# Loading the second and third group's queries and keys when the attention begins instead of within the projections

## The reference

```python
# layer 0: 16 heads of 16 numbers, causal
q, k, v = (proj(Wq), proj(Wk), proj(Wv))
q = q * cos + _rotate_half(q) * sin
k = k * cos + _rotate_half(k) * sin
scores = jnp.where(causal, min, einsum('bhqd,bhkd->bhqk', q, k) * scale)
out = einsum('bhqk,bhkd->bhqd', softmax(scores), v)
x = _layernorm(x + out @ Wo.T)
...
# layer 1: 16 pairs of heads of 8 numbers, not causal, rotary positions as well
attn1, attn2 = attend(q1, k1), attend(q2, k2)
a = attn1 - lam * attn2          # then an rms norm per head, and Wo
```

## Time and profile before

| | us |
|---|---|
| median of 3 runs | 3674.9 |
| lowest, highest | 3674.15, 3680.14 |
| the profiled execution, its own time | 3676.61 |
| its span, first to last instruction | 3674.9 |

### The profile page before, as it was taken

How to read it: one execution, slowest core, us unless ns; L and a number is a source line. 1 busy time by engine, 2 the same in 40 slices (tenths; PEclk the granted TensorE clock), 3 DMA queues, 4 the chain that set the end, 5 groups by cost and what they waited for, 6 DMA issues and landing times. The chain is left out here.

```text
span 3674.9 us, 63919 instructions
## 1 busy us (share of the span) xinstructions
PE 3200.6 (87%) x23832; PEld 1634.2 (44%) x23832; DVE 2804.8 (76%) x4740; ACT 2064.6 (56%) x4079; POOL 911.8 (25%) x1343
## 2 busy tenths in 40 slices
PE   7499999688598979999999999998567699998749
PEld 4244444444486523333333333333434354554626
DVE  7688884557577999999999999993654577775475
ACT  3078887155232339999999999998122133333110
POOL 4234344134333500000000000001144344444000
PEclk9689999788699969999999999999778799999679
DMA  5412220000000601010100101000012311100202
GB/s 179 124 40 69 54 55 22 23 1 1 24 1 21 187 25 28 20 28 20 28 20 20 27 20 28 20 20 4 9 57 91 119 29 45 48 2 4 98 20 81
DMA packets 77548, 157.14 MB, mean 43 GB/s; under 512 B 21336, under 2 KB 38752, under 8 KB 77120
## 3 DMA queue, kind: packets, MB, share of 16 engines
q1 hardware_dynamic: 73024, 148.97, 13.6%
q10 hardware_dynamic: 4224, 4.19, 0.3%
HBM read 87.76 MB, written 54.72 MB: 39 GB/s over the span
## 5 line engine op out<-in xcount | busy, mean ns | idle before, releaser
L600 ACT ACTIVATE L_parts<-L_attn_psS 128x512 f32<-128x512 f32 (+3 forms) x2816 | 1408.2, 574 | 138.1 <-PE L_attn_psS L727 100.7
L683 DVE TENSOR_REDUCE L_attn_tops<-L_attn_psM 128x2 f32<-128x1024 f32 x1152 | 1324.4, 1214 | 51.9 <-PE L_attn_psM L777 47.9
L777 PE MATMUL L_attn_psM<-L_K,L_Q 30*128 30x512 f32 (+4 forms) x2816 | 863.9, 488 | 62.5 <-DVE L_attn_tops L683 35.3
L727 PE MATMUL L_attn_psS<-L_Q,L_K 32*128 32x512 f32 (+4 forms) x2816 | 875.3, 472 | 2.0 <-ACT L_parts L600 0.7
L748 PE MATMUL L_attn_psS<-L_parts,L_attn_V 128*32 128x256 f32 (+1 forms) x10752 | 847.8, 387 | 5.8 <-ACT L_parts L600 0.6
L727 PEld LDWEIGHTS L_attn_psS<-L_Q,L_K 32*128 32x128 f32 (+1 forms) x2816 | 409.6, 184 | 548.3 <-ACT L_parts L600 258.3
L777 PEld LDWEIGHTS L_attn_psM<-L_K,L_Q 30*128 30x128 f32 (+1 forms) x2816 | 391.3, 189 | 109.5 <-DVE L_attn_tops L683 67.1
L748 PEld LDWEIGHTS L_attn_psS<-L_parts,L_attn_V 128*32 128x32 f32 x10752 | 214.4, 108 | 351.4 <-issue 182.1
L677 DVE CUSTOM_DVE_ANT_0 L_attn_psM<-L_attn_psM,L_attn_wide 128x384 f32<-128x384 f32 (+3 forms) x512 | 236.3, 521 | 18.8 <-PE L_attn_psM L777 18.2
L2312 ACT ACTIVATE x_E<-x_psS 128x512 f32<-128x512 f32 x256 | 138.9, 595 | 183.1 <-PE x_psS L2435 173.1
L2358 DVE TENSOR_REDUCE x_tops<-x_psM 128x2 f32<-128x1024 f32 x128 | 153.2, 1206 | 91.4 <-PE x_psM L2464 91.3
(11 more groups left out here) (343 smaller groups left out, 4093.4 us busy)
## 6 DMA issues: line engine op xcount, KB each, us to landing
parts_q<-L_parts SPq DMA_DIRECT2D x64, 256.0 KB
parts_k<-L_parts SPq DMA_DIRECT2D x64, 256.0 KB
L_Q<-parts_q SPq DMA_DIRECT2D x192, 64.0 KB
L_K<-parts_k SPq DMA_DIRECT2D x192, 64.0 KB
L_Q<-parts_q SPq DMA_DIRECT2D x64, 128.0 KB
L_K<-parts_k SPq DMA_DIRECT2D x64, 128.0 KB
queries<-x1p_qo SPq DMA_DIRECT2D x16, 512.0 KB
keys<-x1p_ko SPq DMA_DIRECT2D x16, 512.0 KB
```

Of the source, the lines that this page charges most:

```text
L600: act.activation(E[(4 * n + s) % (4 * RING)][:, c0:], psS[bank][:, c0:], ACT.Exp, scale=scale).then_inc(e_done, 1)
L683: dve.tensor_reduce(dst, src, AX, ALU.max).then_inc(m_read, 1)
L727: pe.matmul(psS[bank][:, c0:], K[g.slot][r:r + RH, c, kt * P:(kt + 1) * P], Q[g.slot][r:r + RH, c, q * HALF + c0:(q + 1) * HALF], start=Tr ...
L777: last = pe.matmul(psM[bank][:, j * HALF:j * HALF + n], Q[t.slot][r:r + TOP, c, qt * P:(qt + 1) * P], K[t.slot][r:r + TOP, c, h * HALF:h * ...
```

## The change

Between the halves of `project`, only group 0 is loaded, 16 DMAs instead of 48. In `attend`, SP's turns 1 and 2 also call `load_group`, without the two waits that the later groups have (the wait for `parts_out` stays at group 3, that for `s_done` at group 3 and later). So group 1 is loaded right after the mask (and in layer 1 the lambdas) are issued, since SP has nothing else in turn 0, and group 2 after the eight small DMAs of group 0's maxima. This holds for both layers.

```diff
--- before.py
+++ after.py
@@ -217,8 +217,7 @@
                         sp.wait_ge(blank, 6)
                         for k in range(4):
                             sp.wait_ge(out[k], OUT)
-                        for g in range(3):
-                            load_group(sp, keep, 2 * ne, g)
+                        load_group(sp, keep, 2 * ne, 0)
 
             @block.gpsimd
             def _(pool):
@@ -492,11 +491,12 @@
                     sp.dma_start(lam4[:], a[f"{tag}_lambda"].rearrange("(o k) d -> o k d", o=1).broadcast_to([P, 4, dh])).then_inc(lamin, 16)
 
                 def turn(t, new, last, old):
-                    if new and t.base >= 3:
+                    if new and t.base >= 1:
                         if t.base == 3:
                             for k in range(4):
                                 sp.wait_ge(parts_out[k], 256)
-                        sp.wait_ge(s_done, s_at[t.base - 3, NS - 1, 3] + 1)
+                        if t.base >= 3:
+                            sp.wait_ge(s_done, s_at[t.base - 3, NS - 1, 3] + 1)
                         load_group(sp, keep, dh, t.base)
                     if last:
```

## The result

| | before | after |
|---|---|---|
| median, us | 3680.64 (19 runs) | 3670.04 (19 runs) |
| lowest to highest | 3673.09 to 3693.76 | 3645.66 to 3687.77 |
| ratio, 95% interval | | 0.9965, 0.9952 to 0.9978 |
| the profiled execution's span | 3674.9 | 3669.7 |

By the ratio the change makes the kernel faster by 0.35%, 0.22 to 0.48%: about 12.9 us, between 8 and 18; the medians are 10.6 us apart. Forecast were 17.6 us and a time of 3657.3, in a range of 3652 to 3663; the measured 3670.04 lies outside. The miss of 12.7 us has two parts: the kernel before is at 3680.64 over 19 runs and not at the 3674.9 of the first three (5.7 us), and the difference of the medians is 10.6 us and not 17.6 (7.0 us).

The account below looks back on a forecast made before the run. The prediction took layer 0's second-half store drain, lengthened by loads ahead of it, as the bound. Layer 0's 16.4 us plus layer 1's 1.2 made 17.6, off the 3674.9 median: 3657.3 us, range 3652 to 3663.

Parts of the forecast that it names:

- The stores' drain gates the attention of layer 0: Layer 0: the first maxima start only once eight buffers of stores are drained; the change gains 16.4 us there.
- production has room to spare: Layer 0, second half: production and store issue allow the attention near 122, nearly 10 us before the drain at 131.6.
- ACT's stall is a symptom: Layer 0, unit 24: ACT's 18.98 us wait comes from the same queue, does not set the start, and shrinks to 0.4.
- the moved loads are covered: Attention: group 1 has 21 us of cover and group 2 has 19, so moving their loads costs nothing.
- layer 1 is worth about 1 us: Layer 1's projections: DVE's loss of 1.2 us is gained, with ends of nothing and 3.7 us.
- absorbed: Rival: the mask is late for its own reason or loads slow stores far more; gain under 7.3 us, 3668 to 3675; 4%.
- late loads: Rival: PE stands at turn 1 because group 1 has not landed, costing its lateness; landing at 186 gives 3682; 2%.
- the mask falls behind: Rival, layer 0: group 1's loads served beside the mask; total gain 9.4 us, 3665.5; sign: mask landing near 141; 6%.
- the stores are drained only at 91.6 + 40.0 = 131.6: Layer 0: store engines finish group 0's loads at 91.6, then need 40.0 us for 8.39 MB at 211 GB/s.
- The bound taken for slower stores: Layer 0, attention's begin: beside group 1's loads the stores fall to 157 GB/s for 8.2 us and lose 2.1 us.
- stores below 200 GB/s after 122: Layer 0, changed profile: named as a sign that the forecast is wrong, by contention.
- The attention begins near 122: Layer 0: production ends at 118.9, the last four stores' issue at 121.3, and the engines need 0.7 us to meet.

Follow-up runs that it names:

- half_stores: Changed kernel with half of layer 0's second-half stores left out (4.2 MB instead of 8.4), its last eight groups' loads reading the first eight's rows; 0.9923 of the kernel before.
- two_groups: Changed kernel with groups 0 and 1 loaded between the halves and group 2 in the attention, in both layers; ratio 0.9981 to the kernel before.
- load_after_four: Changed kernel with group 0's load moved behind the fourth buffer of the second half; ratio 0.9968 to the kernel before.
- spare_loads: Changed kernel with groups 1 and 2 also loaded between the halves, on their own semaphore, and again in the attention; ratio 1.0010 to the kernel before.
- after_again: The changed kernel measured and profiled again without an edit; ratio 0.9953 to the kernel before.

## Why the prediction was wrong in size

**What held.** The stores' drain gates the attention of layer 0 (half_stores), the loads between the halves stand ahead of it in the queue at about 8 us for a group (two_groups, 7.6 us), production has room to spare, ACT's stall is a symptom (load_after_four), the moved loads are covered (spare_loads, and no wait of PE), and layer 1 is worth about 1 us. The rivals "absorbed" and "late loads" did not happen. Nor did "the mask falls behind", although the mask, used at 143.48, came near the 141 that was its sign: in the four profiles with the change in layer 0 the mask is used 5.1 to 5.8 us after its issue, and in the two of two_groups, where no load stands right behind it, 5.3 and 6.0.

**The step that failed** is the one that carried the drain over: "the stores are drained only at 91.6 + 40.0 = 131.6". The 40.0 us were 8.39 MB at 211 GB/s, a rate read from 108 to 148 us, behind 25 us of loads, and from 70 to 80 us. It was taken over as fixed. In the four profiles with the change in layer 0 the same stores ran at 166 to 186 GB/s. That the rate is not fixed was to be had in the trace of before, in the view by stretches:

```profile
40.00:70.00 30.00, 30.00 (x107) 18.15 (x106) 28.97 (x44) 12.26 (x22) 18.76 (x12) 1.00 0.50 179
```

That is 179 GB/s at nearly the same share, and in steps of 5 us between 40 and 80 us the rate runs from 152 to 213. The row hints and no more: production supplies there at most a buffer in 5.6 us (two units of 2.8 us), 1.05 MB / 5.6 us = 187 GB/s. But 179 as the other bound would have given 8.39 MB / 179 GB/s = 46.9 us and a gain in layer 0 of 9.5 us. At the mean of the four profiles with the change in layer 0, (184 + 185 + 166 + 186) / 4 = 180 GB/s, the drain takes 46.6 us, 6.6 more than forecast: 16.4 - 6.6 = 9.8 us for layer 0. The traces show 69.6 - 60.7 = 8.9 us there and about 1 us in layer 1, together 9.9. The interval of the first comparison, 8 to 18 us, holds that; the one of after_again (11 to 23 us) lies just above it, and holds the forecast 17.6. So the time alone would not convict the sum; the profiles do, and some us of the measured gain are not placed in a stage. The bound taken for slower stores, 2.1 us for the time in which group 1's loads run beside them, was of another cause and too small. The sign "stores below 200 GB/s after 122" did show (184 GB/s from 110 to 135 us), but not by contention with group 1's loads: the first of them is issued behind the mask, after 137.95.

**A second step was wrong and cost nothing.** "The attention begins near 122": SP's issuing was costed at the first profile's 4.90 us for eight stores. It takes 8.7 to 12.6 us in most profiles, as fast as the queue drains, so the engines meet at 137 and wait for the mask another 5 us instead of 11.

**The base.** The forecast time stood on a median of three runs, 3674.9; the same kernel had medians of 3676 to 3685 in the later comparisons. Single runs of the changed kernel spread over 42 us, with the granted clock: 3645.66 at a mean clock of 0.914, 3687.77 at 0.904. A range of 11 us in absolute time was too narrow for that: even the forecast gain would have given 3680.64 - 17.6 = 3663.0, the range's upper end. The ratio was forecast at 0.9952, which is the edge of the first interval.

"Faster", at 94%, came true. The cause of the rate itself stays open: why the same stores, from the same buffers to the same rows, move 180 GB/s at one time and 210 at another with their engines equally busy.

## What to carry to other kernels

When one queue is the bound, cost a removal by what the queue will do once the removed work is gone, and give the sum a bound for each rate that the trace shows for the same transfers, not only for the highest. A long stall that ends on a DMA is often the shadow of a drain: moving it away (here with a load 25 us later, or with the mask out of the queue) changes little or nothing until the bytes ahead of the gate change. Move the loads that have some 20 us of cover, and leave the one that the next stage opens with where it is.

## What was not expected of the hardware

- The same 8.39 MB of stores moved at 166 to 193 GB/s or at 198 to 210, with the DMA share at 0.49 to 0.52 in both; long loads ahead of them went with the higher rate in all but one profile, but stores with no load ahead reached 202 to 211 as well in six profiles (70 to 80 us).
- In layer 0 the stores fill only half the DMA share (0.52), in layer 1 they reach 0.89 and 283 GB/s (kernel before, 1264 to 1290 us). Their destination's slowest dimension is 8 in layer 0 and 16 in layer 1, which agrees with what the Trainium skill says (DMA: Bandwidth & Descriptors, Why a DMA increments its semaphore by 16 and not by 1) on how many engines a DMA gets: the largest number up to 16 that divides the slowest dimensions of both sides. No run here changed the layout to test it.
- SP issues the last stores of 256 KB of layer 0 in 0.6 us each in two of the profiles of before and in 1.1 to 1.6 us in the others, which is the pace of the drain. What lets it run ahead in the two is open.
